# Cross attention of a Perceiver kernel: mixes in blocks of four chunks, and K split into high and low by GpSimd

## The chip, the cores and the metric

The kernel runs on one core of a Trainium2 chip. The metric is the device time of one execution in microseconds; a kernel's time is the median of its runs. The engines are TensorE (PE, with its weight loads PEld), VectorE (DVE), ScalarE (ACT), GpSimd (POOL) and SyncE (SP), which issues the transfers.

## The reference

Two layers of a Perceiver in float32, with 256 latent rows of 512 values and a context of 25088 rows of 512. Each layer is a cross attention to the context, a self attention and a mixture of experts, each on the layer norm of x and added to x. What the change touches is the cross attention of layer 1:

```python
Q = (layernorm(x) @ Wq + bq)          # 256 x 16 heads x 32
K = ctx @ Wk + bk                     # 25088 x 16 x 32
V = ctx @ Wv + bv
scores = einsum('bihd,bjhd->bijh', Q, K) / sqrt(32)
attn = softmax(scores, axis=1)        # over the 256 latent rows i, not over the context
x = x + einsum('bijh,bjhd->bihd', attn, V).reshape(...) @ Wo + bo
```

The softmax runs over the latent rows, so each context row j has a maximum and a sum of its own for every head, and the context can be worked through once.

## The kernel before

The kernel goes through the layers in order. First it sums the context for layer 0 and computes a part of V in advance (kept in memory, v_scr), then self attention and experts of layer 0, the cross attention of layer 1, and self attention and experts of layer 1. Each engine has a program of its own, written out by hand; engines meet on semaphores, and `w.wait_ge(name, n)` waits on one, unless that value was awaited before. Products that need more than one pass of TensorE's fast float32 form (float32r) split both operands into a high part and the rest, and add three products (`PASSES`).

The cross attention of layer 1 runs in 784 chunks. A context of 25088 rows is 98 groups g of 256 rows (`GT`), or 196 tiles t of 128 rows. Chunk k is tile t = k // 4 and four heads, c = k % 4. Eight chunks make a group. What happens for chunk k:

- TensorE, `scores(k, half)`: two matmuls of 128x128 weights (`STK`) and 256 columns (`QS`), one for each of two heads, into one half of the two PSUM bank pairs that chunks use in turn (banks 0 and 1, or 2 and 3). K's high and low parts are stacked in the contraction of `STK`, so one pass does. They wait for the exps of chunk k - 2, which read that bank.
- VectorE, `maxima(k, half)`: minus the maximum over the 256 latent rows, into `nm` (L1111).
- ScalarE, `exps(k, half)`: two ACTIVATEs into `EE` with their sums in `su` (L774).
- VectorE, `reciprocals(k)` (L1117), after the maxima of chunk k + 1. GpSimd, `scale_v(k)` (L1348): the tile of V for these heads, times the reciprocals, into `VS`.
- TensorE, `mix(k)` (L583): for four heads a product of 32 columns of weights (`VS`) with 256 columns of `EE`, in plain float32, added up in banks 6 and 7 over all tiles. One chunk leaves eight records.

`EE`, `VS`, `nm`, `su` and `rc` have four places, taken by k % 4. Beside this each loop has the work for later groups. For even k TensorE does `project_k` (L550): 12 matmuls for a quarter `ch` of K of group k // 8 + 2 into bank 4. ScalarE writes K with its bias to `KHL` as float32r, which is the high part (`k_hi`, L765), and VectorE bank 4 plus bias minus the high part (`k_lo`, L1098). For odd k it does `project_v` (L563), a third of a tile of V in bank 5, emptied by VectorE's `v_out` (L1107); a third of the tiles comes from v_scr instead. Once per group, at k % 8 == 5, VectorE casts the next group's context (`split_hi`, L1088) and GpSimd subtracts (`split_lo`, L1337).

SyncE, in one queue: `load_ctx` (L288, a group's context), `stack_k(g + 2)` at the end of group g (L306, 16 transfers that bring `KHL` into the order of `STK`; they wait for the group's K and for its scores, since `STK` has two places) and `fetch_v` (L314).

TensorE's order is scores(k, 0), K or V work, scores(k, 1), and after odd k from 3 on mix(k - 3) and mix(k - 2). K's work waits for k_lo of the quarter before it, because bank 4 is single. VectorE's order in turn k is maxima(k, 0), k_lo of chunk k - 1's K if there was one, maxima(k, 1), v_out, reciprocals(k - 1), split_hi. GpSimd's is scale_v(k - 1), split_lo.

Of the kernel before, what the change touches and what calls it, by code (L numbers as in the profile page):

```python
# [7 lines left out]
P = 128  # L8
F32 = mybir.dt.float32
F32R = mybir.dt.float32r  # L10
ALU = mybir.AluOpType
# [18 lines left out]
BSLOT = [0, 1, 2, 3, 0, 1, 2]  # L30
NPC = 32

PASSES = ((0, 0), (0, 1), (1, 0))
# [8 lines left out]
f0_xs f0_hi f0_lo f0_up f0_silu f0_mul f0_hhi f0_hlo f0_dn f0_acc gate_mm gate_sig gate_comb  # L42
ctx_hi ctx_lo kp_mm k_hi k_lo q_mm q_out q_split vp_mm v_out s_mm s_max s_exp s_rcp vs mix_mm ot_dve ot_act xo_mm x_xo x_xbias
f1_xs f1_hi f1_lo f1_up f1_gelu f1_hhi f1_hlo f1_dn f1_acc g1_mm g1_sub g1_exp g1_comb g1_turn g1_pt b2_mm b2_out y_mv y_rstd y_out
# [51 lines left out]
def build(nc, a):  # L96
    ctx = ExitStack()
    with ctx:
# [45 lines left out]
        V = sb("V", [P, 4, D], over=life)  # L144
        VS = sb("VS", [P, 4, P], over=life)
        EE = sb("EE", [P, 4, 4, 256], over=life)
        OT = sb("OT", [P, NC, 256], over=life)
        WO = sb("WO", [P, NC, D], over=life)
        QHL = sb("QHL", [P, 2, NC, 256], F32R, life)
        life.close()  # L150
# [62 lines left out]
        qf = EE[:, 3].rearrange("p c i -> p (c i)")  # L213
        nm = small[:, 0:16].rearrange("p (b s) -> p b s", b=4)
        su = small[:, 16:32].rearrange("p (b s) -> p b s", b=4)
        rc = small[:, 32:48].rearrange("p (b s) -> p b s", b=4)
        KBANK = (6, 2, 3, 4)

        lng, lnb = LN[:, 0], LN[:, 1]
# [8 lines left out]
        def sync_program(e):  # L228
# [68 lines left out]
            e.dma_start(wqx, a["l1x"][:, 0:2048].rearrange("p (c n) -> p c n", c=NC)).then_inc(S["d_wx"], 16)  # L297
            e.dma_start(WO[:, :, :], a["l1x"][:, 2048:4096].rearrange("p (c n) -> p c n", c=NC)).then_inc(S["d_wo"], 16)

            def stack_k(g):  # L300
                w.wait_ge("k_lo", 4 * g + 4)
                if g >= 2:
                    w.wait_ge("s_mm", 16 * (g - 2) + 16)
                for s in range(4):
                    for q in range(4):
                        e.dma_start(  # L306
                            STK[32 * q:32 * q + 32, g % 2, s, :, :].bitcast(F32),
                            KHL[32 * s:32 * s + 32, g % 2, q % 2, :, :].bitcast(F32)).then_inc(S[f"d_s{g % 2}"], 16)
# [18 lines left out]
            for k in range(NCH):  # L327
# [6 lines left out]
                if k % 8 == 5 and g + 6 < NG:  # L334
                    load_ctx(g + 6)

            def load_piece(n):
# [20 lines left out]
        def tensor_program(e):  # L358
# [220 lines left out]
            def mix(k):  # L579
                t, c, b = k // 4, k % 4, k % 4  # L580
                w.wait_ge("vs", k + 1)
# [26 lines left out]
            for k in range(NCH):  # L608
                scores(k, 0)
                if due_k(k):  # L610
                    g, ch = due_k(k)
                    w.wait_ge("k_lo", 4 * g + ch)
                    project_k(g, ch)
                elif due_v(k):
                    project_v(*due_v(k))
                scores(k, 1)
                if k % 2 and k >= 3:
                    mix(k - 3)
                    mix(k - 2)
            mix(NCH - 2)  # L620
# [68 lines left out]
        def scalar_program(e):  # L689
# [71 lines left out]
            def k_hi(g, ch, kb=4):  # L761
                w.wait_ge("kp_mm", 4 * g + ch + 1)
                if g >= 2 and ch == 0:
                    w.wait_ge(f"d_s{g % 2}", 256 * (g // 2))
                e.activation(KHL[:, g % 2, 0, ch, :], bank(kb, 0, GT), ACT.Identity,  # L765
                             bias=BC[:, C_L1XK + ch:C_L1XK + ch + 1]).then_inc(S["k_hi"], 1)

            def exps(k, half):
                b = k % 4
                w.wait_ge("s_max", 2 * k + half + 1)  # L770
                if k >= 4:
                    w.wait_ge("mix_mm", k - 3)
                for s in (2 * half, 2 * half + 1):
# [9 lines left out]
            for k in range(NCH):  # L783
                exps(k, 0)
                if due_k(k):
                    k_hi(*due_k(k))
                exps(k, 1)
# [36 lines left out]
        def vector_program(e):  # L824
# [271 lines left out]
            def k_lo(g, ch, kb=4):  # L1096
# [3 lines left out]
                    in1=KHL[:, g % 2, 0, ch, :].bitcast(F32), op0=ALU.add, op1=ALU.subtract).then_inc(S["k_lo"], 1)  # L1100

            def v_out(n):
                t = v_tile(n)
# [5 lines left out]
            def maxima(k, half):  # L1109
                w.wait_ge("s_mm", 2 * k + half + 1)  # L1110
                e.tensor_reduce(  # L1111
                    nm[:, k % 4, 2 * half:2 * half + 2], bank(2 * (k % 2) + half).rearrange("p (s i) -> p s i", s=2),
                    axis=AX.X, op=ALU.max, negate=True).then_inc(S["s_max"], 1)

            def reciprocals(k):
                w.wait_ge("s_exp", 2 * k + 2)
                e.reciprocal(rc[:, k % 4, :], su[:, k % 4, :]).then_inc(S["s_rcp"], 1)  # L1117

# [26 lines left out]
            for k in range(NCH):  # L1145
                maxima(k, 0)
                if k and due_k(k - 1):
                    k_lo(*due_k(k - 1))
                maxima(k, 1)
# [103 lines left out]
        def gpsimd_program(e):  # L1253
# [87 lines left out]
            def scale_v(k):  # L1341
                b, t, c = k % 4, k // 4, k % 4
                w.wait_ge("s_rcp", k + 1)
                if v_count(t):
                    w.wait_ge("v_out", v_count(t))
                else:
# [4 lines left out]
                    rc[:, b, :].unsqueeze(2).to_broadcast([P, 4, 32]), ALU.mult).then_inc(S["vs"], 1)  # L1351

            split_lo(2)
            for k in range(NCH):
                if k >= 1:
                    scale_v(k - 1)
                if k % 8 == 5 and k // 8 + 3 < NG:
                    split_lo(k // 8 + 3)
# [97 lines left out]
```

## Time and profile before

| | us |
|---|---|
| median of 3 runs | 2800.24 |
| lowest and highest | 2800.18, 2800.51 |
| profiled execution | 2798.85 |
| its span | 2797.0 |
| mean granted clock of TensorE | 0.983 |

| engine | busy us | share of the span |
|---|---|---|
| TensorE matmul | 2690.8 | 96% |
| TensorE weight load | 2199.8 | 79% |
| ScalarE | 2007.4 | 72% |
| VectorE | 1964.5 | 70% |
| GpSimd | 822.3 | 29% |

The first scores of layer 1's cross attention start at 554.3 us and its last mix at 2331.8 us. A timeline's row gives start and duration in us, engine, line, operation, the tile written and those read, and how many instructions were merged into it. Matmuls are pipelined: a row's duration contains the time to fill the array, so the distance from one row's start to the next is what a group of them occupies, and rows overlap. "idle before" is the engine's idle time with what ended it. In a group of instructions the numbers behind the bar are busy us in all, mean ns of one, and idle time before them.

### The profile page before, as it was taken

Reading aid. Unit: us, or ns where it says so; the run is one execution under the profiler, and the core shown is the slowest. Engines: PE = TensorE matmul, PEld = TensorE weight load, DVE = VectorE, ACT = ScalarE, POOL = GpSimd, SP = SyncE. Lnnn points to the kernel's source line nnn. Section 1 sums busy time; section 2 is a strip of 40 time slices with the busy share of each in tenths; the row PEclk is TensorE's granted clock in tenths of the full one; section 3 lists DMA queues with packets and bytes.
Section 4 is the critical chain, followed back from the end, with each engine's and each line's share of the span. In section 5 each row is a group of like instructions: output and inputs, shape, how many; then the busy total and the mean of one; then the engine's idle time right before and its main releaser. Section 6 shows DMA issues by size and latency. Waiting matters only on the chain.

```text
span 2797.0 us, 58526 instructions
## 1 busy us (share of the span) xinstructions
PE 2690.8 (96%) x21096; PEld 2199.8 (79%) x21096; DVE 1964.5 (70%) x3785; ACT 2007.4 (72%) x7206; POOL 822.3 (29%) x1138
## 2 busy tenths in 40 slices
PE   7998799899999999999999999999999998899998
PEld 5775799777777777787777877778777775699997
DVE  6775766577777777777777777777777775555555
ACT  2112444299999999999999999999999995255543
POOL 4431111133333333333333333333333321122222
PEclk9999899999999999999999999999999998899999
DMA  9983445456665656666565666656566652354451
GB/s 340 387 318 155 159 170 202 121 145 167 158 156 149 158 151 152 167 157 153 150 161 147 157 166 155 152 152 159 148 159 160 160 125 101 145 195 182 181 184 65
DMA packets 132147, 473.26 MB, mean 169 GB/s; under 512 B 31112, under 2 KB 31240, under 8 KB 124688
## 3 DMA queue, kind: packets, MB, share of 16 engines
q1 hardware_dynamic: 131856, 469.52, 57.5%
q8 instruction: 166, 2.72, 0.4%
q14 instruction: 125, 1.02, 0.1%
HBM read 244.47 MB, written 17.30 MB: 94 GB/s over the span
## 4 chain that ended last, share of the span: by engine, by line
PE 85%; DVE 6%; POOL 5%; issue 2%; DMA 2%; ACT 1%; SPq 0%; POOLq 0%
PE PB L550 18%; PE PB L575 14%; PE PB L583 12%; PE PB L563 11%; PE PB L643 7%; PE PB L659 6%; PE PB L511 5%; PE PB L387 5%; POOL CTX L1337 3%; PE PB L524 3%; DVE small L1111 2%; POOL VS L1348 1%; DMA AR<-in_ctx 1%; PE PB L415 1%; DVE V L1107 1%
## 5 line engine op out<-in xcount | busy, mean ns | idle before, releaser
L774 ACT ACTIVATE EE<-PB,small 128x256 f32<-128x256 f32 x3136 | 1446.0, 482 | 131.4 <-DVE small L1111 117.9
L1111 DVE TENSOR_REDUCE small<-PB 128x2 f32<-128x512 f32 x1568 | 1062.5, 678 | 439.7 <-PE PB L575 439.2
L1348 POOL TENSOR_TENSOR VS<-V,small 128x128 f32<-128x128 f32 x784 | 347.9, 444 | 1207.1 <-DVE small L1117 1207.1
L774 ACT ACTIVATION_READ_ACCUMULATOR EE<-PB,small 128x1 f32 x3136 | 663.6, 212 | 0.0
L575 PEld LDWEIGHTS PB<-QS,STK 128*128 128x128 f32 x3136 | 480.5, 190 | 202.3 <-issue 163.4
L550 PE MATMUL PB<-CTX,WKV 128*128 128x256 f32 x4704 | 624.9, 282 | 4.0 <-DVE CTX L1092 2.6
L575 PE MATMUL PB<-QS,STK 128*128 128x256 f32 x3136 | 605.6, 295 | 6.1 <-ACT EE L774 3.3
L550 PEld LDWEIGHTS PB<-CTX,WKV 128*128 128x128 f32 x4704 | 588.7, 190 | 4.8 <-DVE CTX L1092 3.1
L583 PE MATMUL PB<-EE,VS 128*32 128x256 f32 x6272 | 426.6, 386 | 8.4 <-POOL VS L1348 8.4
L563 PE MATMUL PB<-WKV,CTX 128*128 128x512 f32 x1584 | 432.4, 395 | 0.8 <-DVE V L1107 0.8
L563 PEld LDWEIGHTS PB<-WKV,CTX 128*128 128x128 f32 x1584 | 272.9, 190 | 36.9 <-DVE V L1107 1.2
L583 PEld LDWEIGHTS PB<-EE,VS 128*32 128x32 f32 x6272 | 160.1, 109 | 138.5 <-POOL VS L1348 25.0
L1337 POOL TENSOR_TENSOR CTX<-RAW,CTX 128x1024 fp32r<-128x1024 f32 x96 | 230.1, 2397 | 27.1 <-DVE CTX L1088 27.1
L643 PEld LDWEIGHTS PB<-XS,WS 128*128 128x128 f32 x1536 | 204.0, 194 | 17.2 <-issue 6.9
L643 PE MATMUL PB<-XS,WS 128*128 128x256 f32 x1536 | 207.5, 286 | 5.0 <-DVE WS L1178 5.0
L765 ACT ACTIVATE KHL<-PB,BC 128x256 fp32r<-128x256 f32 x392 | 185.6, 474 | 27.3 <-PE PB L550 27.3
L659 PE MATMUL PB<-WS,HS 128*128 128x512 f32 x768 | 198.3, 394 | 0.0
L808 ACT ACTIVATE HF<-PB,MS 128x256 f32<-128x256 f32 x128 | 61.1, 477 | 184.7 <-PE PB L643 184.7
L387 PE MATMUL PB<-WKV,CS 128*128 128x512 f32 x768 | 180.6, 397 | 10.9 <-POOL CS L1302 10.9
L1098 DVE SCALAR_TENSOR_TENSOR KHL<-PB,BC,KHL 128x256 fp32r<-128x256 f32 x392 | 186.2, 475 | 4.0 <-ACT KHL L765 4.0
L1178 DVE TENSOR_TENSOR WS<-RW,WS 128x1024 fp32r<-128x1024 f32 x128 | 165.5, 1333 | 25.7 <-ACT WS L802 25.7
L1365 POOL TENSOR_TENSOR HS<-HF,HS 128x256 fp32r<-128x256 f32 x128 | 101.0, 789 | 279.3 <-DVE HS L1185 279.3
(194 smaller groups left out, 2193.4 us busy)
## 6 DMA issues: line engine op xcount, KB each, us to landing
STK<-KHL SPq DMA_DIRECT2D x1568, 128.0 KB, 2.8
RW<-in_l1f SPq DMA_DIRECT2D x32, 2048.0 KB, 8.1
AR<-in_ctx SPq DMA_DIRECT2D x49, 1024.0 KB, 8.7
RAW<-in_ctx SPq DMA_DIRECT2D x98, 512.0 KB, 4.2
WF<-in_l0f SPq DMA_DIRECT2D x17, 2304.0 KB, 8.6
v_scr<-RAW SPq DMA_DIRECT2D x64, 256.0 KB, 8.1
V<-v_scr SPq DMA_DIRECT2D x64, 256.0 KB, 2.9
WA<-in_l0a SPq DMA_DIRECT2D x1, 4096.0 KB, 12.9
```

Of the source, the lines that this page charges most:

```text
L387: m = e.matmul(bank(5 + r % 3), CS[:, q % 3, xh, c, j:j + 128], WKV[:, 2 + wh, c, :], start=(z == 0 and c == 0), stop=(z == 2 and c == 3))
L550: m = e.matmul(bank(kb, 0, GT), WKV[:, wh, c, 128 * ch:128 * ch + 128], CTX[:, g % 3, xh, c, :], start=(z == 0 and c == 0), stop=(z == 2 a ...
L563: m = e.matmul(bank(5), CTX[:, g % 3, xh, c, j:j + 128], WKV[:, 2 + wh, c, :], start=(part == 0 and c == 0), stop=(part == 2 and c == 3))
L575: m = e.matmul(bank(2 * (k % 2) + half, 256 * (s % 2), 256), STK[:, g % 2, s, c, j:j + 128], QS[:, s, c, :], start=True, stop=True)
L583: m = e.matmul(PB[32 * s:32 * s + 32, 6 + c // 2, 256 * (c % 2):256 * (c % 2) + 256], VS[:, b, 32 * s:32 * s + 32], EE[:, b, s, :], start= ...
L643: m = e.matmul(bank(n % 4, 0, 256), w1[:, c, 128 * f:128 * f + 128], XS1[:, xh, c, :], start=(z == 0 and c == 0), stop=(z == 2 and c == 3))
L659: m = e.matmul(bank(4 + 2 * (x % 2) + i), HS1[:, n % 4, hh, 128 * i:128 * i + 128], w2[:, f, :], start=(fc == 0 and z == 0), stop=(fc == 1 ...
L774: m = e.activation(EE[:, b, s, :], bank(2 * (k % 2) + half, 256 * (s % 2), 256), ACT.Exp, bias=nm[:, b, s:s + 1], accum_out=su[:, b, s:s + 1])
L1098: e.scalar_tensor_tensor(out=KHL[:, g % 2, 1, ch, :], in0=bank(kb, 0, GT), scalar=BC[:, C_L1XK + ch:C_L1XK + ch + 1], in1=KHL[:, g % 2, 0, ...
L1111: e.tensor_reduce(nm[:, k % 4, 2 * half:2 * half + 2], bank(2 * (k % 2) + half).rearrange("p (s i) -> p s i", s=2), axis=AX.X, op=ALU.max, ...
L1337: e.tensor_tensor(CTX[:, g % 3, 1, :, :].rearrange("p c j -> p (c j)"), RAW[:, g % 3, :], CTX[:, g % 3, 0, :, :].rearrange("p c j -> p (c ...
L1348: e.tensor_tensor(VS[:, b, :].rearrange("p (s d) -> p s d", s=4), V[:, t % 4, 128 * c:128 * c + 128].rearrange("p (s d) -> p s d", s=4), r ...
```

## The change

Three things, all in the cross attention of layer 1.

- TensorE mixes after every fourth chunk, k % 4 == 3, the four chunks k - 5 to k - 2 (two the first time). The places of `EE`, `VS`, `nm`, `su` and `rc` grow from four to six (`RING`), and exps(k) waits for mix(k - 6).
- K leaves bank 4 by one VectorE instruction, `k_raw`, that adds the bias and writes float32 to a new tile `KR` with two places. It stands where k_lo stood. GpSimd, in turn k + 2, copies `KR` to the high part of `KHL` and subtracts for the low part (`split_k`). ScalarE's k_hi and VectorE's k_lo go in the loop; for the first two groups, before the loop, they stay. TensorE's K work waits for kr_out, SyncE's stack_k for kr_lo.
- `QHL` lies where `WO` is, and `WO` is loaded at k = 40 in place of ahead of the loop.

```diff
@@ -29,6 +29,8 @@
 R_L0X, R_L0V, R_L0O, R_XV, R_XO, R_AV, R_AO = range(7)
 BSLOT = [0, 1, 2, 3, 0, 1, 2]
 NPC = 32
+MIX = 4
+RING = 6
 
 PASSES = ((0, 0), (0, 1), (1, 0))
 
@@ -40,7 +42,7 @@
 wkv_hi wv_dve wv_pool wk_pool sums early_hi early_lo early_mm early_out p1_mm x_bias mean_rhs mean_mm x_mean
 qk_mm qk_out av_mm av_out x_abias sc_mm sc_max sc_exp sc_rcp diag turn_mm turn_out amix_mm amix_out ao_mm x_attn
 f0_xs f0_hi f0_lo f0_up f0_silu f0_mul f0_hhi f0_hlo f0_dn f0_acc gate_mm gate_sig gate_comb
-ctx_hi ctx_lo kp_mm k_hi k_lo q_mm q_out q_split vp_mm v_out s_mm s_max s_exp s_rcp vs mix_mm ot_dve ot_act xo_mm x_xo x_xbias
+ctx_hi ctx_lo kp_mm k_hi k_lo kr_out kr_hi kr_lo q_mm q_out q_split vp_mm v_out s_mm s_max s_exp s_rcp vs mix_mm ot_dve ot_act xo_mm x_xo x_xbias
 f1_xs f1_hi f1_lo f1_up f1_gelu f1_hhi f1_hlo f1_dn f1_acc g1_mm g1_sub g1_exp g1_comb g1_turn g1_pt b2_mm b2_out y_mv y_rstd y_out
 """.split()
 
@@ -142,11 +144,14 @@
         STK = sb("STK", [P, 2, 4, NC, GT], F32R, life)
         QS = sb("QS", [P, 4, NC, 256], F32R, life)
         V = sb("V", [P, 4, D], over=life)
-        VS = sb("VS", [P, 4, P], over=life)
-        EE = sb("EE", [P, 4, 4, 256], over=life)
+        KR = sb("KR", [P, 2, GT], over=life)
+        VS = sb("VS", [P, RING, P], over=life)
+        EE = sb("EE", [P, RING, 4, 256], over=life)
         OT = sb("OT", [P, NC, 256], over=life)
+        q_life = ExitStack()
+        QHL = sb("QHL", [P, 2, NC, 256], F32R, q_life)
+        q_life.close()
         WO = sb("WO", [P, NC, D], over=life)
-        QHL = sb("QHL", [P, 2, NC, 256], F32R, life)
         life.close()
         kv_life.close()
         life = ExitStack()
@@ -211,10 +216,11 @@
 
         wqx = EE[:, 0:2].rearrange("p b s i -> p (b s i)").rearrange("p (c n) -> p c n", c=NC)
         qf = EE[:, 3].rearrange("p c i -> p (c i)")
-        nm = small[:, 0:16].rearrange("p (b s) -> p b s", b=4)
-        su = small[:, 16:32].rearrange("p (b s) -> p b s", b=4)
-        rc = small[:, 32:48].rearrange("p (b s) -> p b s", b=4)
+        nm, su, rc = (small[:, o:o + 4 * RING].rearrange("p (b s) -> p b s", b=RING) for o in (0, 32, 64))
         KBANK = (6, 2, 3, 4)
+
+        def k_done(g, ch):
+            return ("k_lo", 4 * g + ch + 1) if g < 2 else ("kr_lo", 4 * (g - 2) + ch + 1)
 
         lng, lnb = LN[:, 0], LN[:, 1]
         b2 = MS[0:8, 0:512]
@@ -295,10 +301,9 @@
                 load0(x)
             w.wait_ge("f0_acc", 34)
             e.dma_start(wqx, a["l1x"][:, 0:2048].rearrange("p (c n) -> p c n", c=NC)).then_inc(S["d_wx"], 16)
-            e.dma_start(WO[:, :, :], a["l1x"][:, 2048:4096].rearrange("p (c n) -> p c n", c=NC)).then_inc(S["d_wo"], 16)
 
             def stack_k(g):
-                w.wait_ge("k_lo", 4 * g + 4)
+                w.wait_ge(*k_done(g, 3))
                 if g >= 2:
                     w.wait_ge("s_mm", 16 * (g - 2) + 16)
                 for s in range(4):
@@ -333,6 +338,9 @@
                     fetch_v(t + 2)
                 if k % 8 == 5 and g + 6 < NG:
                     load_ctx(g + 6)
+                if k == 40:
+                    w.wait_ge("d_q", 256)
+                    e.dma_start(WO[:, :, :], a["l1x"][:, 2048:4096].rearrange("p (c n) -> p c n", c=NC)).then_inc(S["d_wo"], 16)
 
             def load_piece(n):
                 if n >= 3:
@@ -577,7 +585,7 @@
                 m.then_inc(S["s_mm"], 1)
 
             def mix(k):
-                t, c, b = k // 4, k % 4, k % 4
+                t, c, b = k // 4, k % 4, k % RING
                 w.wait_ge("vs", k + 1)
                 for s in range(4):
                     m = e.matmul(
@@ -609,14 +617,15 @@
                 scores(k, 0)
                 if due_k(k):
                     g, ch = due_k(k)
-                    w.wait_ge("k_lo", 4 * g + ch)
+                    if k:
+                        w.wait_ge("kr_out", 4 * (g - 2) + ch)
                     project_k(g, ch)
                 elif due_v(k):
                     project_v(*due_v(k))
                 scores(k, 1)
-                if k % 2 and k >= 3:
-                    mix(k - 3)
-                    mix(k - 2)
+                if k % MIX == MIX - 1:
+                    for n in range(max(k - MIX - 1, 0), k - 1):
+                        mix(n)
             mix(NCH - 2)
             mix(NCH - 1)
             w.wait_ge("ot_dve", 1)
@@ -760,16 +769,14 @@
 
             def k_hi(g, ch, kb=4):
                 w.wait_ge("kp_mm", 4 * g + ch + 1)
-                if g >= 2 and ch == 0:
-                    w.wait_ge(f"d_s{g % 2}", 256 * (g // 2))
                 e.activation(KHL[:, g % 2, 0, ch, :], bank(kb, 0, GT), ACT.Identity,
                              bias=BC[:, C_L1XK + ch:C_L1XK + ch + 1]).then_inc(S["k_hi"], 1)
 
             def exps(k, half):
-                b = k % 4
+                b = k % RING
                 w.wait_ge("s_max", 2 * k + half + 1)
-                if k >= 4:
-                    w.wait_ge("mix_mm", k - 3)
+                if k >= RING:
+                    w.wait_ge("mix_mm", k - RING + 1)
                 for s in (2 * half, 2 * half + 1):
                     m = e.activation(EE[:, b, s, :], bank(2 * (k % 2) + half, 256 * (s % 2), 256), ACT.Exp,
                                      bias=nm[:, b, s:s + 1], accum_out=su[:, b, s:s + 1])
@@ -782,8 +789,6 @@
                 k_hi(1, ch, kb)
             for k in range(NCH):
                 exps(k, 0)
-                if due_k(k):
-                    k_hi(*due_k(k))
                 exps(k, 1)
             w.wait_ge("mix_mm", NCH)
             e.activation(OT[:, 2:4, :].rearrange("p c i -> p (c i)"), bank(7), ACT.Copy).then_inc(S["ot_act"], 1)
@@ -1099,6 +1104,14 @@
                     out=KHL[:, g % 2, 1, ch, :], in0=bank(kb, 0, GT), scalar=BC[:, C_L1XK + ch:C_L1XK + ch + 1],
                     in1=KHL[:, g % 2, 0, ch, :].bitcast(F32), op0=ALU.add, op1=ALU.subtract).then_inc(S["k_lo"], 1)
 
+            def k_raw(g, ch):
+                n = 4 * (g - 2) + ch
+                w.wait_ge("kp_mm", 4 * g + ch + 1)
+                if n >= 2:
+                    w.wait_ge("kr_lo", n - 1)
+                e.tensor_scalar(KR[:, n % 2, :], bank(4, 0, GT), BC[:, C_L1XK + ch:C_L1XK + ch + 1], None,
+                                ALU.add).then_inc(S["kr_out"], 1)
+
             def v_out(n):
                 t = v_tile(n)
                 w.wait_ge("vp_mm", n + 1)
@@ -1109,12 +1122,12 @@
             def maxima(k, half):
                 w.wait_ge("s_mm", 2 * k + half + 1)
                 e.tensor_reduce(
-                    nm[:, k % 4, 2 * half:2 * half + 2], bank(2 * (k % 2) + half).rearrange("p (s i) -> p s i", s=2),
+                    nm[:, k % RING, 2 * half:2 * half + 2], bank(2 * (k % 2) + half).rearrange("p (s i) -> p s i", s=2),
                     axis=AX.X, op=ALU.max, negate=True).then_inc(S["s_max"], 1)
 
             def reciprocals(k):
                 w.wait_ge("s_exp", 2 * k + 2)
-                e.reciprocal(rc[:, k % 4, :], su[:, k % 4, :]).then_inc(S["s_rcp"], 1)
+                e.reciprocal(rc[:, k % RING, :], su[:, k % RING, :]).then_inc(S["s_rcp"], 1)
 
             split_hi(0)
             split_lo(0)
@@ -1145,7 +1158,7 @@
             for k in range(NCH):
                 maxima(k, 0)
                 if k and due_k(k - 1):
-                    k_lo(*due_k(k - 1))
+                    k_raw(*due_k(k - 1))
                 maxima(k, 1)
                 if due_v(k) and due_v(k)[1] == 2:
                     v_out(due_v(k)[0])
@@ -1339,7 +1352,7 @@
                                 ALU.subtract).then_inc(S["ctx_lo"], 1)
 
             def scale_v(k):
-                b, t, c = k % 4, k // 4, k % 4
+                b, t, c = k % RING, k // 4, k % 4
                 w.wait_ge("s_rcp", k + 1)
                 if v_count(t):
                     w.wait_ge("v_out", v_count(t))
@@ -1350,10 +1363,22 @@
                     V[:, t % 4, 128 * c:128 * c + 128].rearrange("p (s d) -> p s d", s=4),
                     rc[:, b, :].unsqueeze(2).to_broadcast([P, 4, 32]), ALU.mult).then_inc(S["vs"], 1)
 
+            def split_k(g, ch):
+                n = 4 * (g - 2) + ch
+                w.wait_ge("kr_out", n + 1)
+                if ch == 0:
+                    w.wait_ge(f"d_s{g % 2}", 256 * (g // 2))
+                e.tensor_copy(KHL[:, g % 2, 0, ch, :], KR[:, n % 2, :]).then_inc(S["kr_hi"], 1)
+                w.wait_ge("kr_hi", n + 1)
+                e.tensor_tensor(KHL[:, g % 2, 1, ch, :], KR[:, n % 2, :], KHL[:, g % 2, 0, ch, :].bitcast(F32),
+                                ALU.subtract).then_inc(S["kr_lo"], 1)
+
             split_lo(2)
             for k in range(NCH):
                 if k >= 1:
                     scale_v(k - 1)
+                if k >= 2 and due_k(k - 2):
+                    split_k(*due_k(k - 2))
                 if k % 8 == 5 and k // 8 + 3 < NG:
                     split_lo(k // 8 + 3)
             scale_v(NCH - 1)
```

## Rows read from the trace of the kernel before

**Rows 1.** The page: the chain's shares by engine, then a group of instructions

```profile
PE 85%; DVE 6%; POOL 5%; issue 2%; DMA 2%; ACT 1%; SPq 0%; POOLq 0%
...
L575 PEld LDWEIGHTS PB<-QS,STK 128*128 128x128 f32 x3136 | 480.5, 190 | 202.3 <-issue 163.4
```

**Rows 2.** Windows: stretch, busy us of PE, PEld, DVE, ACT, POOL, clock, DMA

```profile
1000.00:2000.00 1000.00, 996.35 (x8809) 794.19 (x8812) 750.85 (x1672) 929.33 (x3743) 323.75 (x496) 1.00 0.61 156
```

**Rows 3.** Timeline of TensorE, two stretches of the loop

```profile
1495.36 0.40 PE L575 MATMUL PB<-QS,STK 128*128 128x256 f32 x2
...
1500.19 0.64 PE L583 MATMUL PB<-EE,VS 128*32 128x256 f32 x8
1501.02 0.64 PE L583 MATMUL PB<-EE,VS 128*32 128x256 f32 x8 [0.19 <-POOL VS L1348]
1501.59 0.50 PE L575 MATMUL PB<-QS,STK 128*128 128x256 f32 x2
1501.93 1.59 PE L550 MATMUL PB<-CTX,WKV 128*128 128x256 f32 x12
1503.36 0.64 PE L575 MATMUL PB<-QS,STK 128*128 128x256 f32 x4
1503.84 1.09 PE L563 MATMUL PB<-WKV,CTX 128*128 128x512 f32 x4
1504.77 0.40 PE L575 MATMUL PB<-QS,STK 128*128 128x256 f32 x2
1505.10 1.07 PE L583 MATMUL PB<-EE,VS 128*32 128x256 f32 x16
1506.10 0.50 PE L575 MATMUL PB<-QS,STK 128*128 128x256 f32 x2
```

**Rows 4.** Timeline of TensorE in the tail without K work

```profile
2311.93 0.50 PE L575 MATMUL PB<-QS,STK 128*128 128x256 f32 x2 [0.32 <-ACT EE L774]
2312.27 1.09 PE L563 MATMUL PB<-WKV,CTX 128*128 128x512 f32 x4
```

**Rows 5.** Timeline of VectorE in the same pair of chunks

```profile
1503.81 0.69 DVE L1111 TENSOR_REDUCE small<-PB 128x2 f32<-128x512 f32 x1 [0.98 <-PE PB L575]
...
1504.50 0.66 DVE L1111 TENSOR_REDUCE small<-PB 128x2 f32<-128x512 f32 x1
1505.08 0.47 DVE L1098 SCALAR_TENSOR_TENSOR KHL<-PB,BC,KHL 128x256 fp32r<-128x256 f32 x1
```

**Rows 6.** Groups by form: the nearest forms to the new instructions

```profile
L902 DVE TENSOR_SCALAR AR<-PB,BC 128x256 f32<-128x256 f32 x4 | 1.9, 477 | 1.6 <-PE PB L415 1.6
...
L1365 POOL TENSOR_TENSOR HS<-HF,HS 128x256 fp32r<-128x256 f32 x128 | 101.0, 789 | 279.3 <-DVE HS L1185 279.3
...
L1273 POOL MEMSET mask<- 128x256 f32 x1 | 0.3, 312 | 0.1
...
L1185 DVE CAST HS<-HF 128x256 fp32r<-128x256 f32 x128 | 37.3, 292 | 131.8 <-ACT HF L808 131.8
```

**Rows 7.** Timeline of GpSimd: scale_v around the same pair

```profile
1497.49 0.76 POOL L1348 TENSOR_TENSOR VS<-V,small 128x128 f32<-128x128 f32 x1 [1.85 <-DVE small L1117]
...
1500.57 0.40 POOL L1348 TENSOR_TENSOR VS<-V,small 128x128 f32<-128x128 f32 x1
...
1504.66 0.40 POOL L1348 TENSOR_TENSOR VS<-V,small 128x128 f32<-128x128 f32 x1 [2.86 <-DVE small L1117]
```

**Rows 8.** Timeline of ScalarE in the same pair

```profile
1503.33 0.47 ACT L774 ACTIVATE EE<-PB,small 128x256 f32<-128x256 f32 x1
```

**Rows 9.** Waits, 560 to 2296 us: total us, times, longest

```profile
PEld PB L583 <- POOL VS L1348: 21.6, 32, 0.7
```

**Rows 10.** SyncE's queue, then one line's time to landing

```profile
1501.07 10.03 SPq L306 DMA_DIRECT2D STK<-KHL  x16
...
1519.10 11.20 SPq L306 DMA_DIRECT2D STK<-KHL  x16
...
DMA to landing us min/median/max: 2.3/2.8/4.1
```

## The prediction

> **What bounds the kernel now.** I read the page first, then the cross attention loop only, because the edit touches nothing else. TensorE makes 85% of the chain that ended last [rows 1], so I ask of every part what it does to TensorE. The loop over the 784 chunks (t, c) fills 560 to 2296 us and then a tail without K work. In it TensorE is busy for 996 of 1000 us at full clock, ScalarE for 929, VectorE for 751, GpSimd for 324 [rows 2]. Busy hides what matters here, so I went on to the timeline of TensorE and read starts, not durations. The loop repeats exactly. One pair of chunks from 1501.59 to 1506.10 is 4.51 us: two score matmuls, 12 of K (project_k), four scores, four of V (project_v), two scores, 16 records of the mixes (eight a chunk) [rows 3]. I write S(k,h) for the scores of chunk k, half h, and call four chunks a quad; it lasts 9.02 us now.
>
> **What the longer mix block saves.** From S(1,1) at 1504.77 to the next K at 1506.44 are 1.67 us: four scores and a block of two mixes. Four scores in a row take 0.48 (1503.36 to 1503.84), so the block costs 1.19. A block of 8 records has 0.64 and one of 16 has 1.07 [rows 3], so one more chunk in a block costs 0.43 and two cost 0.86. Putting two pairs of mixes in one block therefore saves 1.19 - 0.86 = 0.33 us a quad: the gaps around the change between full matmuls and 32-column ones. K work ends with chunk 768, that is 192 quads; behind it TensorE waits for ScalarE anyway [rows 4], and there nothing is won. With the first quad, which has no mix, left out: 191 x 0.33 = 63 us.
>
> **What the missing mixes uncover.** In the middle of a quad S(2,0) and the second K follow S(1,1) directly. That K writes bank 4, and waits until VectorE has emptied it of the first K. Before, the mixes lay between. VectorE's order is untouched: maxima(0,1), reciprocals, maxima(1,0), then the K instruction, then maxima(1,1). The trace gives that path: S(0,1) starts at 1503.36 [rows 3], the maxima at 1503.81, the next maxima at 1504.50, K's instruction at 1505.08, for 0.47 [rows 5]: bank 4 is free at 1505.55. It cannot begin earlier, for S(0,1) stands behind the first K on TensorE, and VectorE idles 0.98 us for it. What replaces k_lo there is k_raw, a TENSOR_SCALAR from PSUM of 128x256; L902 has that form at 477 ns [rows 6] against the 0.47 of k_lo. So nothing is gained on this path, although ScalarE loses k_hi: ScalarE is not on it.
> TensorE would be ready for the second K at 1503.36 + 0.48 + 0.93 (V, 1503.84 to 1504.77) + 0.48 = 1505.25. It gets it at 1505.55 plus 0.05 (a scale_v of 0.40 from 1500.57 let TensorE go at 1501.02 [rows 3, 7]), that is 0.35 late. After such a wait the first weights are not loaded ahead: in the tail the stalled pair of scores takes 0.34 to the next group (2311.93 to 2312.27) [rows 4] where 0.24 is half of four unstalled ones. I add 0.10, between 0 and 0.19 (one weight load of L575, [rows 1]). Delay 0.45, saving 0.33: the quad becomes **0.12 longer**, 9.14 us; 191 x 0.12 = +23 us. Everything behind the wait is queued on TensorE: the second K, S(2,1), V, S(3,1), the mixes.
>
> **ScalarE and the six places.** ScalarE is busy for 929 of 1000 us [rows 2] with k_hi, 8.4 us of a quad of 9.1, and less without it: that saves work off the path, 0. S(2,0) needs exps(0,0), whose second instruction ends at 1503.80 [rows 8], with its accumulator some 2.4 us after S(0,0); S(2,0) comes 3.4 after. exps(k) waits for mix k-6; the block behind S(3,1) mixes up to k-2, so the mix needed is always one block old: 0. VectorE trades one instruction for one of the same length.
>
> **The waits of mixes for scale_v.** 32 mix blocks wait for GpSimd now [rows 9], in the groups (eight chunks) where v_out, split_hi and split_lo come together: the block at 1500.19 takes 1.40 in place of 1.00, 0.40 lost. scale_v(5) stands behind split_lo and ends at 1500.97 [rows 7], 5.61 us after S(5,1) at 1495.36 [rows 3]. In the new order it is the fourth chunk of its block. With S(5,1) at quad time 1504.77 it is ready at 1510.38 + 0.05. The block begins at 1505.70 + 1.43 + 0.48 + 0.93 + 0.32 = 1508.86, its fourth chunk some 1.33 later, 1510.19. So 0.24 of 0.40 stay, 32 x 0.16 = -5 us (0 to -13).
>
> **GpSimd's split of K.** It adds per K one copy and one subtraction. The subtraction is the form of L1365, 789 ns. For the copy no row has the form: bounds are a MEMSET of 128x256, 312 ns, and the two-input 789 [rows 6]. I take 0.45, nearer the memset, since one stream is read and written. The Trainium skill (GPSIMD Engine Reference, Engine selection) has one-input operations at roughly VectorE's line rate and two-input ones about 2x slower. By VectorE's cast of 128x256, 292 ns [rows 6], the estimate by that page is 0.3 for the copy, and the term of the stack below would shrink to nil.
> GpSimd is busy for 324 of 1000 us now [rows 2], 5.8 of a group's 18.0; four splits of 1.3 make it 11 of 18.3. split_k stands behind scale_v(k-1) in its turn, and the next scale_v waits for a later reciprocal, so the mixes don't see it. What queues behind it is SP: **stack_k**. Now it starts at 1501.07, 0.52 before S(8,0) at 1501.59 [rows 3, 10]. Then the last split of a group waits for scale_v(7), which runs 1504.66 to 1505.06 [rows 7], + 0.45 + 0.79 + 0.15 of signals: 1506.45, 4.9 us after S(8,0), 5.4 later than now. 16 issues take 10.03 to 11.20 us, 0.63 each, and a landing comes 2.8 behind its issue [rows 10]: 12.2 to 13.4. It lands 17.1 to 18.3 after S(8,0), and S(16,0) wants it after 18.3. The 5 us of slack are spent to between 1.1 and 0: I take +3 us for the groups with late landings (0 to +10). fetch_v and load_ctx stand behind stack_k on SP's queue; they serve chunks eight and more later.
> The load of WO leaves the prologue, where nothing waits for it: 0.
>
> **The sum.** +23 - 5 + 3 = +21 us. The profiled execution is 2798.85 (span 2797.0), so 2820 for it; the median of the runs is 2800.24, so **2821**.
>
> **Rivals.**
> (a) The second K does not wait: VectorE frees bank 4 in time. For it: the trace of before shows no TensorE wait for VectorE in the loop; those for GpSimd are its longest in that list [rows 9]. Against it: that path is four fixed rows. Then the quad is 8.69 and the group 17.4, shorter than the 17.1 to 18.3 of the stack, which takes back some 0.3 a group: -63 - 13 + 30 = -46, **2754**.
> (b) The switches save as computed, but the wait has no refill and the scale_v waits go wholly: 191 x 0.02 - 13 = -9, with 2 for the stack **2793**, at the edge of no change.
> (c) Slower by the stack: if copy and subtraction take over 1.2 us more than I think, or the transfers are slowed, S(8g,0) waits for d_s in every group, and the group becomes the stack's loop. It decides from a stack start later than about 6 us after S(8g,0) by the shorter row. At 0.5 us a group: 98 x 0.5 = 49 on top of 21, **2870**. The trace has one contention to offer: scale_v at 1497.49 took 0.76 in place of 0.40 [rows 7] while VectorE's cast ran. The Trainium skill (Advanced Engine Details and Errata, VectorE Performance Modes) says that two-port Vector instructions and GpSimd's block each other. By that rule, the trace agrees, a split could be stretched by 0.4 once in a group, but no cast falls on the last split of a group.
> (d) The change doesn't do what it says: if k_raw were delayed by kr_lo (two places in KR), bank 4 would be held longer. split n-2 is done 4 us before k_raw n: hardly any chance, inside (c).
>
> **Chances.** Forecast 0.68, (a) 0.12, (b) 0.10, (c) with (d) 0.10. The bounds of the forecast: the lowest values of all terms give -9, which is (b); a full refill of 0.19, nothing saved on scale_v and 10 for the stack give 191 x 0.21 + 10 = +50. I take (b) in and close the top at twice the forecast's loss, +42, so that 2 in 10 stay out, (a) and most of (c): **2790 to 2842**. A measurement tells about 0.2% (5.6 us) from no change. Faster by more: (a) and half of (b), 0.17. Within: the other half and the forecast's low edge, 0.12. Slower: 0.71.
>
> **What would show it.** Right: in the changed kernel's TensorE timeline blocks of 32 mix records lasting 1.86 to the next scores, and within each quad a second K group that starts 2.24 us after the four scores before V, not 1.89, with k_raw named as what ended the wait; pairs of quads of 18.3 us; ScalarE 10 points less busy; GpSimd near 60%. stack_k starting 4.9 us after a group's first scores. Wrong: K groups that follow S(2,0) without a gap (rival a); scores of a group's first chunk waiting for a DMA in most groups (c); waits for GpSimd in more than one block of six, which I excluded; or k_raw, or the copy, of other length than taken here.

## The result and the profile after

The changed kernel takes 2815.94 us (median of four runs, 2815.03 to 2817.18) where the kernel before took 2800.21 in the same session: a ratio of 1.0056, 95% interval 1.0039 to 1.0074. It is slower by 15.7 us; 2821 was forecast. The span of the profiled execution went from 2797.0 to 2813.7, by 16.7 us.

TensorE's timeline over one quad, as start, duration, engine, line, operation and count; L583 are the scores now, L558 K, L571 V, L591 the mixes:

```profile
1502.04 0.50 PE L583 MATMUL PB<-QS,STK 128*128 128x256 f32 x2
1502.38 1.59 PE L558 MATMUL PB<-CTX,WKV 128*128 128x256 f32 x12
1503.81 0.64 PE L583 MATMUL PB<-QS,STK 128*128 128x256 f32 x4
1504.29 1.09 PE L571 MATMUL PB<-WKV,CTX 128*128 128x512 f32 x4
1505.21 0.63 PE L583 MATMUL PB<-QS,STK 128*128 128x256 f32 x4
1506.05 1.69 PE L558 MATMUL PB<-CTX,WKV 128*128 128x256 f32 x12 [0.20 <-DVE KR L1112]
1507.57 0.64 PE L583 MATMUL PB<-QS,STK 128*128 128x256 f32 x4
1508.05 1.09 PE L571 MATMUL PB<-WKV,CTX 128*128 128x512 f32 x4
1508.98 0.40 PE L583 MATMUL PB<-QS,STK 128*128 128x256 f32 x2
1509.31 2.20 PE L591 MATMUL PB<-EE,VS 128*32 128x256 f32 x32
1511.43 0.50 PE L583 MATMUL PB<-QS,STK 128*128 128x256 f32 x2
...
1518.71 1.93 PE L591 MATMUL PB<-EE,VS 128*32 128x256 f32 x32
1520.57 0.50 PE L583 MATMUL PB<-QS,STK 128*128 128x256 f32 x2
```

It is the loop of [rows 3] with one mix block where two stood. The quad from 1511.43 to 1520.57 lasts 9.14 us against 9.02. Its mixes take 1.86 to the next scores (1518.71 to 1520.57), as summed. The second K starts 2.24 us behind the four scores in front of V (1503.81 to 1506.05), and its row names what it waited for, K's instruction on VectorE. The row gives only 0.20 of idle time, because it counts from the modelled end of the matmuls before. The starts tell more: the four scores in front of that K take 0.84 to it (1505.21 to 1506.05) and would take 0.47.

VectorE over the same stretch, where [rows 5] stood:

```profile
1504.24 0.69 DVE L1124 TENSOR_REDUCE small<-PB 128x2 f32<-128x512 f32 x1 [0.98 <-PE PB L583]
1504.85 0.17 DVE L1130 RECIPROCAL small<-small 128x4 f32<-128x4 f32 x1
1504.94 0.66 DVE L1124 TENSOR_REDUCE small<-PB 128x2 f32<-128x512 f32 x1
1505.52 0.47 DVE L1112 TENSOR_SCALAR KR<-PB,BC 128x256 f32<-128x256 f32 x1
```

Spacing and durations are those of before: k_raw ends at 1505.99, and TensorE goes on at 1506.05. Now the list of waits over the loop with K work (total us, times, longest):

```profile
PEld PB L558 <- DVE KR L1112: 76.6, 191, 0.4
PE PB L558 <- DVE KR L1112: 37.5, 191, 0.2
PEld PB L591 <- POOL VS L1361: 17.2, 32, 0.5
PEld PB L583 <- DMA STK<-KHL: 6.2, 14, 0.8
```

The wait for k_raw occurs 191 times, the count of the forecast, and was not in the list of the kernel before at all. The waits of mixes for GpSimd are still 32 [rows 9]. 14 groups wait a little for the stack, the transfers that fill `STK`. In the windows table (columns as in [rows 2]) TensorE is down from 996 to 977 of 1000 us, ScalarE by 100, GpSimd up by 226:

```profile
1000.00:2000.00 1000.00, 977.22 (x8718) 795.83 (x8718) 739.91 (x1651) 829.82 (x3488) 549.98 (x926) 1.00 0.63 154
```

### The profile page after: what moved, and what is told of

The parts are those of the page before. It is cut to its first block, busy times and chain, and to the rows that moved or that the text cites. A ratio compares the mean times of both kernels' runs of the same rounds, so it can differ in the third digit from the quotient of the medians.

```text
span 2813.7 us, 59195 instructions
## 1 busy us (share of the span) xinstructions
PE 2671.9 (95%) x21096; PEld 2215.7 (79%) x21096; DVE 1960.2 (70%) x3785; ACT 1848.6 (66%) x6822; POOL 1228.7 (44%) x1906
## 4 chain that ended last, share of the span: by engine, by line
PE 77%; DVE 13%; POOL 4%; issue 3%; DMA 1%; SPq 1%; ACT 1%; POOLq 0%
PE PB L558 20%; PE PB L591 11%; PE PB L583 10%; PE PB L652 7%; PE PB L571 7%; PE PB L668 6%; DVE small L1124 6%; PE PB L519 5%; PE PB L395 5%; POOL CTX L1350 3%; PE PB L532 2%; DVE KR L1112 2%; POOL VS L1361 1%; DVE small L1130 1%; DMA AR<-in_ctx 1%
## 5 line engine op out<-in xcount | busy, mean ns | idle before, releaser
L558 PE MATMUL PB<-CTX,WKV 128*128 128x256 f32 x4704 | 643.3, 286 | 40.2 <-DVE KR L1112 37.5
L558 PEld LDWEIGHTS PB<-CTX,WKV 128*128 128x128 f32 x4704 | 585.0, 189 | 79.8 <-DVE KR L1112 76.6
L583 PEld LDWEIGHTS PB<-QS,STK 128*128 128x128 f32 x3136 | 468.8, 190 | 128.6 <-issue 65.8
L583 PE MATMUL PB<-QS,STK 128*128 128x256 f32 x3136 | 555.0, 288 | 11.6 <-ACT EE L781 5.0
L571 PE MATMUL PB<-WKV,CTX 128*128 128x512 f32 x1584 | 432.4, 395 | 0.8 <-DVE V L1120 0.8
L591 PE MATMUL PB<-EE,VS 128*32 128x256 f32 x6272 | 387.4, 384 | 1.8
L571 PEld LDWEIGHTS PB<-WKV,CTX 128*128 128x128 f32 x1584 | 272.9, 190 | 37.0 <-DVE V L1120 1.2
L1373 POOL TENSOR_TENSOR KHL<-KR,KHL 128x256 fp32r<-128x256 f32 x384 | 280.8, 731 | 30.7
L591 PEld LDWEIGHTS PB<-EE,VS 128*32 128x32 f32 x6272 | 180.8, 110 | 140.0 <-POOL VS L1361 18.0
L1112 DVE TENSOR_SCALAR KR<-PB,BC 128x256 f32<-128x256 f32 x384 | 181.7, 473 | 0.0
```

Of the source, the lines that this page charges most:

```text
L558: m = e.matmul(bank(kb, 0, GT), WKV[:, wh, c, 128 * ch:128 * ch + 128], CTX[:, g % 3, xh, c, :], start=(z == 0 and c == 0), stop=(z == 2 a ...
L571: m = e.matmul(bank(5), CTX[:, g % 3, xh, c, j:j + 128], WKV[:, 2 + wh, c, :], start=(part == 0 and c == 0), stop=(part == 2 and c == 3))
L583: m = e.matmul(bank(2 * (k % 2) + half, 256 * (s % 2), 256), STK[:, g % 2, s, c, j:j + 128], QS[:, s, c, :], start=True, stop=True)
L591: m = e.matmul(PB[32 * s:32 * s + 32, 6 + c // 2, 256 * (c % 2):256 * (c % 2) + 256], VS[:, b, 32 * s:32 * s + 32], EE[:, b, s, :], start= ...
L1373: e.tensor_tensor(KHL[:, g % 2, 1, ch, :], KR[:, n % 2, :], KHL[:, g % 2, 0, ch, :].bitcast(F32), ALU.subtract).then_inc(S["kr_lo"], 1)
```

## The experiments

Each edit below is against the changed kernel. Theory: the second K of a quad pays for the moment at which bank 4 is emptied, which the order of VectorE's work sets; K's detour over GpSimd is neither the loss nor, in this kernel, a gain. Rivals: the detour itself costs, through GpSimd or the stack; or ScalarE falls behind. The lists of waits in this section run from 560 to 2250 us, which leaves out the last chunks with K work where a loop is longer.

### Each half of the change alone

**Mixes alone**, with K on its old way by k_hi and k_lo (the waits of TensorE, ScalarE and SyncE go back to k_lo with it and are left out here):

```diff
-                    k_raw(*due_k(k - 1))
+                    k_lo(*due_k(k - 1))
...
                 exps(k, 0)
+                if due_k(k):
+                    k_hi(*due_k(k))
                 exps(k, 1)
...
-                if k >= 2 and due_k(k - 2):
-                    split_k(*due_k(k - 2))
```

> The mixes of four chunks and the six places alone; K leaves PSUM as before, by ScalarE's k_hi and VectorE's k_lo, behind maxima(k, 0). Theory: k_lo frees bank 4 at the same moment as k_raw, so the second K waits the same 0.45 us, quads are 9.13 and the kernel takes 2812 to 2818, with stack_k starting early again. Rival 1 (the loss comes from the detour over GpSimd): the quads are 8.69 to 8.8 and the kernel takes 2730 to 2745. Rival 2 (ScalarE, with k_hi on it, falls behind without the mixes between): slower than 2825.

2815.24 us, ratio 1.0058 (1.0043 to 1.0073): the changed kernel's time without any of K's detour. K waits in the same place for the same 2.24 us, now for k_lo. TensorE's timeline of this kernel:

```profile
1503.87 0.64 PE L583 MATMUL PB<-QS,STK 128*128 128x256 f32 x4
...
1505.28 0.63 PE L583 MATMUL PB<-QS,STK 128*128 128x256 f32 x4
1506.11 1.69 PE L558 MATMUL PB<-CTX,WKV 128*128 128x256 f32 x12 [0.20 <-DVE KHL L1106]
```

So the whole slowdown belongs to the mixes of four, and the first rival falls. The second falls too: ScalarE has all its old work here, and the time is the same.

**The detour alone**, mixes two at a time:

```diff
-MIX = 4
+MIX = 2
```

> K's new way out of PSUM and the six places alone; mixes go two at a time as before. Theory: with a block of mixes between every two K groups no K waits; pairs of 4.51 us as before. The late start of stack_k uses up its slack, 18.03 us a group against 16.9 to 18.2 needed: 0 to 3 us in all. 2800 to 2804. Rival (GpSimd's split costs by itself, through stack_k or scale_v): 2810 or more, with many scores waiting for the stack.

2800.06 us, ratio 1.0003 (0.9993 to 1.0012): no difference. Its waits over the loop show the stack where the forecast put it:

```profile
PEld PB L591 <- POOL VS L1361: 20.9, 31, 0.7
PEld PB L583 <- DMA STK<-KHL: 15.4, 35, 0.8
PE PB L583 <- DMA STK<-KHL: 0.5, 2, 0.3
```

35 groups wait for the transfers, nearly all for less than the time in which TensorE still works off what it has: 0.5 us of matmul idle time in all. The slack is used up and no more. Both halves keep the six places and the later load of WO, so these cost nothing either.

### Taking the wait away

The direct test, a second bank for K, was not tried: all eight banks are taken. Two orders free the one bank earlier.

**k_raw ahead of the maxima**, so that bank 4 is free 0.6 us sooner:

```diff
-                maxima(k, 0)
                 if k and due_k(k - 1):
                     k_raw(*due_k(k - 1))
+                maxima(k, 0)
```

> The changed kernel with one move: VectorE's k_raw stands ahead of maxima(k, 0) in place of behind it, so that bank 4 is free about 1.6 us after the scores in front of V, and not 2.2. Theory (the second K of each quad pays 0.45 us for k_raw): no TensorE wait for k_raw, quads of 8.69 us where nothing else holds them. But stack_k still starts 4.6 us after a group's first scores and lands 12.2 to 13.4 later, against a group of now 17.4: in about half of the groups the first scores wait for it, groups average 17.8, the kernel takes 2755 to 2765. Rival (the wait is not what costs, something else fills the quad, as the stack or ScalarE): quads stay at 9.13, within 5 us of 2816.

2760.19 us, ratio 0.9864 (0.9849 to 0.9879). One exchange of two instructions turns the loss into a gain of 39 us, and takes 56 off the changed kernel. No K waits any more; what is left in its list of waits over the loop:

```profile
PEld PB L591 <- POOL VS L1361: 56.3, 95, 1.0
...
PEld PB L583 <- DMA STK<-KHL: 29.1, 50, 1.1
...
PE PB L583 <- DMA STK<-KHL: 6.2, 16, 0.7
```

The stack now holds 50 groups, as expected, and the time lies within the theory's range. But mixes wait for scale_v in 95 of the 96 groups, and that was not expected: with the quad shorter, scale_v(5) behind split_lo is too late in all of them, not in one of three.

**k_raw on ScalarE**, where k_hi stood, is another way to empty the bank early:

```diff
-                    k_raw(*due_k(k - 1))
+                    pass
...
                 exps(k, 0)
+                if due_k(k):
+                    k_raw(*due_k(k))
                 exps(k, 1)
```

(k_raw as an ACTIVATE of form Identity with the bias.)

> The changed kernel with k_raw on ScalarE, between exps(k, 0) and exps(k, 1) where k_hi stood, and nothing of it on VectorE; split_k as in the changed kernel. Theory (only the moment at which bank 4 is free counts): bank 4 is free 0.97 us after the scores in front of V, so no K waits, the quad is 8.69 as with k_raw ahead on VectorE, and the late stack holds groups at 17.7 to 17.8: 2755 to 2765. Rival (ScalarE, busy for 8.4 of 8.7 us, becomes the bound without mixes between): 2775 or more, with scores that wait for exps.

2753.78 us, ratio 0.9831 (0.9816 to 0.9847). That is 1 us under the range of the theory, and far from the rival: the bank emptied early by either engine gives the gain. The moment counts and not the engine. That it is 6 us faster than with k_raw on VectorE fits VectorE's one instruction less in front of the reciprocals that scale_v waits for, but no run separates this.

### The stack and GpSimd's order

**The split earlier**, first alone:

```diff
-                if k >= 1:
-                    scale_v(k - 1)
-                if k >= 2 and due_k(k - 2):
-                    split_k(*due_k(k - 2))
+                if k >= 1 and due_k(k - 1):
+                    split_k(*due_k(k - 1))
+                if k >= 1:
+                    scale_v(k - 1)
```

> The changed kernel with split_k one turn earlier and ahead of scale_v; k_raw stays behind maxima(k, 0). Theory (K's wait holds the quad at 9.13 us, and the late stack costs nearly nothing under it, 0.4 us in all): 2813 to 2818, no measurable gain, though stack_k starts 4 us earlier. Rival (the 3 us that the prediction gave the stack, or more, are there to win): 2806 to 2812.

2832.02 us, ratio 1.0108 (1.0090 to 1.0127): a miss on both expectations, 16 us slower than the changed kernel. stack_k does start about 4 us sooner, and no group waits for it. The waits of the loop tell where the 16 us are:

```profile
POOL KHL L1371 <- DVE KR L1112: 156.5, 274, 5.2
PEld PB L558 <- DVE KR L1112: 73.2, 182, 0.4
PEld PB L591 <- POOL VS L1361: 51.1, 91, 0.6
```

and GpSimd's timeline shows how, before one mix block at 1519.04:

```profile
1515.78 0.40 POOL L1371 CAST KHL<-KR 128x256 fp32r<-128x256 f32 x1 [0.56 <-DVE KR L1112]
1516.26 0.74 POOL L1373 TENSOR_TENSOR KHL<-KR,KHL 128x256 fp32r<-128x256 f32 x1
1517.08 0.76 POOL L1361 TENSOR_TENSOR VS<-V,small 128x128 f32<-128x128 f32 x1
1517.80 2.38 POOL L1350 TENSOR_TENSOR CTX<-RAW,CTX 128x1024 fp32r<-128x1024 f32 x1
```

GpSimd stands still for k_raw, then does the split, and scale_v, split_lo and the next scale_v come that much later. To the end of the loop at 2338 us 95 blocks wait in place of 32. One of them in TensorE's timeline, 2.10 us to the next scores where an unhindered block takes 1.86:

```profile
1500.51 2.17 PE L591 MATMUL PB<-EE,VS 128*32 128x256 f32 x32
1502.61 0.51 PE L583 MATMUL PB<-QS,STK 128*128 128x256 f32 x2
```

That block of each group lasts 2.15 us on average here and 1.96 in the changed kernel: over 96 groups 18.5 of the 19.5 us by which the loop is longer. Against a wait of VectorE's that is late anyway, the change's place for the split, behind scale_v, was the better one. The same move **together with k_raw ahead** of the maxima:

> k_raw ahead of maxima(k, 0), and GpSimd's split_k one turn earlier and ahead of scale_v, so that stack_k starts within 1 us of a group's first scores. Theory: neither K nor the stack waits; groups of 17.4 us and a part of the scale_v waits, 96 x 0.7 = 65 to 75 us less than before: 2728 to 2742. Rival (stack not a bound in the kernel with k_raw ahead): the same time as that kernel within 4 us. Rival (GpSimd's split in front of scale_v makes mixes wait): above 2760.

2750.86 us, ratio 0.9827 (0.9813 to 0.9842): the stack is gone as a bound, 9 us better than with k_raw ahead alone, but 9 worse than the expected end of 2742. The expectation had counted only a part of the scale_v waits; they are in 95 blocks still, and nearly all of the 31 us by which this loop is longer than the next kernel's lie in those blocks:

```profile
PEld PB L591 <- POOL VS L1361: 56.2, 95, 1.0
```

**In addition the context's split two chunks earlier**, so that split_lo lies in front of a scale_v that nobody waits for:

```diff
-                if k % 8 == 5 and k // 8 + 3 < NG:
+                if k % 8 == 3 and k // 8 + 3 < NG:
                     split_hi(k // 8 + 3)
...
-                if k % 8 == 5 and k // 8 + 3 < NG:
+                if k % 8 == 3 and k // 8 + 3 < NG:
                     split_lo(k // 8 + 3)
```

> k_raw ahead of maxima(k, 0), split_k one turn earlier, and in addition split_hi and split_lo at k % 8 == 3 in place of 5, so that split_lo no longer stands in front of the scale_v whose chunk is fourth in the block. Theory (what is left in the kernel without this move, 17.68 us a group against 17.38, are mixes that wait for scale_v): groups of 17.38 to 17.45 us, 96 x 0.25 to 0.3 = 24 to 29 us less than the 2751 of the kernel without the move: 2720 to 2728. Rival (the waits only move, to a K group that waits for ctx_lo or to ScalarE): 2740 to 2755.

2719.80 us, ratio 0.9711 (0.9694 to 0.9729): 80 us less than before, at the lower end of the expectation, and the fastest of all. No mix waits for scale_v any more. Its loop is the bare one that the forecast's rival (a) described, a quad of 8.68 us (1501.99 to 1510.67), as TensorE's timeline shows, and in the windows TensorE is busy throughout:

```profile
1501.99 0.50 PE L583 MATMUL PB<-QS,STK 128*128 128x256 f32 x2
...
1505.16 0.63 PE L583 MATMUL PB<-QS,STK 128*128 128x256 f32 x4
1505.63 1.60 PE L558 MATMUL PB<-CTX,WKV 128*128 128x256 f32 x12
...
1508.80 1.93 PE L591 MATMUL PB<-EE,VS 128*32 128x256 f32 x32
1510.67 0.50 PE L583 MATMUL PB<-QS,STK 128*128 128x256 f32 x2
```

```profile
1000.00:2000.00 1000.00, 1000.00 (x9213) 837.80 (x9213) 780.28 (x1746) 879.85 (x3685) 592.45 (x979) 1.00 0.67 163
```

### Is the detour worth anything?

The fastest kernel with K on its old way, k_lo ahead of the maxima:

```diff
-                maxima(k, 0)
-                if k and due_k(k - 1):
-                    k_raw(*due_k(k - 1))
+                if k and due_k(k - 1):
+                    k_lo(*due_k(k - 1))
+                maxima(k, 0)
```

(with k_hi on ScalarE as in the mixes alone, and split_hi and split_lo at k % 8 == 3.)

> Mixes of four chunks, six places, split_hi and split_lo at k % 8 == 3, and K on its old way (ScalarE's k_hi, VectorE's k_lo) with k_lo ahead of maxima(k, 0): the fastest kernel so far without K's detour over GpSimd. Theory (the detour bought nothing; what counts is the moment bank 4 is free, 1.6 us after the scores in front of V here too): groups of 17.36 us, 2717 to 2725. Rival (ScalarE needs the detour: 16 exps of 0.45 and two k_hi of 0.45 are 8.1 of a quad of 8.68, and where k_hi lies between the exps scores wait for them): groups above 17.5, 2732 or more.

2752.49 us, ratio 0.9835 (0.9819 to 0.9852). The theory's number fails: without the detour the same order is 33 us slower. The waits, and a second K of a quad in TensorE's timeline:

```profile
DVE KHL L1106 <- ACT KHL L773: 207.9, 224, 1.1
PEld PB L583 <- ACT EE L782: 39.5, 96, 0.4
PEld PB L558 <- DVE KHL L1106: 19.0, 33, 0.6
```

```profile
1506.97 1.71 PE L558 MATMUL PB<-CTX,WKV 128*128 128x256 f32 x12
1508.51 0.64 PE L583 MATMUL PB<-QS,STK 128*128 128x256 f32 x4
```

The rival has the time right (2732 or more) and the engine, but not the place: it expected scores to wait for exps, and the scores wait no more than in the fastest kernel (its list has 37.5 us in 86 such waits). ScalarE is busy for 937 of 1000 us here, k_hi comes late behind the exps, VectorE waits for it 224 times, and k_lo frees bank 4 late. By the starts, all of the 35 us by which this loop is longer than the fastest kernel's (1692.5 against 1657.9) lie in the second K of the quads: 19 us in 33 groups that start late, and 16 us because the second K groups take 1.51 us to the next scores on average, as behind a wait (1.54 in the rows), and not 1.43. So it is the wait for the bank again.

The detour is worth nothing while K's wait holds the quad (mixes alone equal the whole change) and 33 us once it doesn't. This holds for k_hi between the two halves of the exps; whether another place for it would free the bank as early was not tried.

## Why the prediction was right

**The saving of the longer block** was right to a hundredth. 1.86 us a block of four was summed and measured, and with nothing in its way the quad is 8.68 against 9.02: 0.34 for 0.33.

**The K wait** was the deciding step and held: VectorE's path was read as 2.19 us from the scores in front of V to a free bank, and K starts after 2.24, 191 times. The refill of 0.10 is there too: the K group takes 1.52 to the next scores (1506.05 to 1507.57) against 1.43 without a wait, unrounded 0.10. Quad 9.14 forecast, 9.14 measured. With the starts unrounded, 9.134 against 9.013, it is 191 x 0.121 = +23.1 us, for +23.

**The mixes' waits for scale_v**: 32 blocks, each 0.26 too long (1509.31 to 1511.43 is 2.12, less 1.86) where 0.24 was reckoned and 0.40 was lost before: -4.4, for -5.

**The stack** was taken too dear, +3 for +0.4. Its start was well placed, 4.65 us after a group's first scores (1511.43 in the fence above) where 4.9 was said, and so was its length, 12.8 us in the middle from the first issue to the last landing (11.8 to 14.0) for 12.2 to 13.4. SyncE's queue:

```profile
1516.08 11.34 SPq L311 DMA_DIRECT2D STK<-KHL  x16
```

The copy on GpSimd takes 397 ns and the subtraction 731, less than the 0.45 and 0.79 taken, which puts GpSimd at 55% in place of near 60%. The estimate of 0.3 for the copy, worked out by the Trainium skill (GPSIMD Engine Reference, Engine selection), is a tenth too short by this trace. Its row and the subtraction's, from the groups of instructions:

```profile
L1373 POOL TENSOR_TENSOR KHL<-KR,KHL 128x256 fp32r<-128x256 f32 x384 | 280.8, 731 | 30.7
...
L1371 POOL CAST KHL<-KR 128x256 fp32r<-128x256 f32 x384 | 152.5, 397 | 0.0
```

The mis-sized part is the price put on late landings: half of the groups had 0.9 us or more left between the last landing and the next group's first scores. That the margin was really spent shows where the quad shrinks: with k_raw ahead, moving the split earlier as well is worth 9 us.

**What the sum left out.** From the first scores of chunk 4 to those of chunk 768 the loop went from 1734.4 to 1753.5 us, +19.1, which is 23.1 - 4.4 + 0.4. The span moved by 16.7. Three pieces lie outside. The start of the loop is 0.5 earlier. The tail of 16 chunks without K, put at no change, is 2.5 us longer (31.7 to 34.2): one late stack there costs 1.6, the last mixes run at the lower clock, as shown below, and the kernel before has waits for GpSimd there that the changed one hasn't; the three were not added up. And everything behind the loop is 4.4 us shorter (464.9 to 460.6), though its code is the same. 2.9 of these lie in the product with WO right behind the loop, 10.07 us before and 7.13 after:

```profile
2333.25 10.07 PE L627 MATMUL PB<-WO,OT 128*128 128x512 f32 x16 [0.81 <-DVE OT L1158]
```

```profile
2348.96 4.54 PE L591 MATMUL PB<-EE,VS 128*32 128x256 f32 x48
2354.32 7.13 PE L636 MATMUL PB<-WO,OT 128*128 128x512 f32 x16 [0.81 <-DVE OT L1171]
```

In the windows from each loop's end on, before and after:

```profile
2332.10:2347.00 14.90, 10.41 (x24) 4.04 (x16) 3.78 (x8) 0.60 (x1) 0.92 (x2) 0.74 0.32 137
```

```profile
2353.10:2368.00 14.90, 9.41 (x32) 4.53 (x24) 5.43 (x11) 0.60 (x1) 0.94 (x2) 0.93 0.30 129
```

The granted clock is 0.74 of full speed before and 0.93 after. Over the product alone it is 0.71 before (2333.20 to 2343.40) and 1.00 after (2354.30 to 2361.50): of the two levels, 1.2 and 2.4 GHz, the lower one fell on a part of the product in the kernel before. In the changed one a stretch of it came earlier, on the last mixes: 0.51 from 2348.90 to 2352.40, and the 48 records take 4.54 us where 32 have 1.93 and 16 more would add 0.86. Kernels with mixes of four all end 3 to 5 us sooner behind their loop, the one with mixes of two (464.2) does not. Ahead of the stretch at the lower level TensorE waited for ScalarE again and again in the changed kernel (2345.80 to 2348.53), but which idleness moved the clock was not tried. Against the forecast's +21 the span has +16.7: 2.6 us less by the stack, 2.4 less outside the loop, 0.7 more by K's wait and scale_v. That the pieces outside the loop nearly cancel is luck.

**The rivals.** (a), no wait, was excluded rightly, and its price for a kernel without the wait, 2754, was met by k_raw ahead (2760) and by k_raw on ScalarE (2754), but by luck: it gave the stack 30 us and let the scale_v waits vanish, where the runs have 9 us for the stack (2760 to 2751, split earlier) and 31 for the scale_v waits (2751 to 2720, split_lo moved). (b) fell with the refill. (c), the stack as the loop's bound, needed a later start than came. "Waits for GpSimd in more than one block of six" would have disproved the forecast; it took 32 of the 192 blocks with K work around them, exactly one in six.

## What to carry to other kernels

Work between two uses of a single buffer can be what hides the emptying of it; before such work is taken out or bundled, follow the path from the first use to the free buffer and compare it with what remains between. Here the gap of 0.33 us a quad was real, and a wait of 0.45 stood behind it. When the wait is gone, the order on the other engines has to be settled again, for each gain exposes the next (stack, scale_v, ScalarE): the same bundling loses 16 us or, after three moves in the order, wins 80, and a part that measures as nothing in one order is worth 33 us in another.

## What the runs showed of the hardware

A return trip between the full 128x128 matmuls and the mixes' 32-column ones costs TensorE 0.33 us: it is the whole difference between two blocks of two and one of four. 0.09 us of it lie in the two scores ahead of a block (0.33 us where 0.24 is usual), 0.10 in the two behind it (0.34), and 0.14 at the ends of the block itself (two blocks of 1.00 against one of 1.86). The Trainium skill (TensorEngine Tiling (Array Packing), Key Properties) says that changing the tiling mode drains TensorE. The trace agrees in that each change costs time; but the mixes are also plain float32 and the work around them float32r, and no run separates the tile's shape from the number format.

The spacing of VectorE's instructions was the same to 0.01 us whether k_lo with a second input from SBUF or k_raw without one stood in the row, and though GpSimd's busy time went up from 324 to 550 of 1000 us. GpSimd's own scale_v did stretch from 0.40 to 0.76 where VectorE's cast of the context ran beside it, in the changed kernels as in [rows 7].
